# Cross-attention kernel: the second half of a tile's output projection runs in one piece ahead of the next tile's output transposes

## The reference

```
query = x @ Wq;  keyt = enc @ Wk;  valt = enc @ Wv
hs = mha(query, keyt, valt)                  # 2048 rows against 150 keys
ca_q1 = einsum('btc,th->bch', ca, Wq_ca)[:, indices, :]
ca_hs1 = mha(ca_q1, x, x)
ca_hs2 = mha(ca_hs1 @ Wq, ca @ Wk_ca, ca @ Wv_ca)
out = (hs + ca_hs2) @ Wout + b_out + x
```

## Time and profile before

| what | value |
|---|---|
| time, median of 3 runs | 1592.3 us (1591.59 to 1593.23) |
| the profiled execution, own time | 1591.01 us |
| its span, first to last instruction | 1589.2 us |
| PE busy | 1530.4 us, 96% of the span |
| PEld busy | 1254.2 us, 79% |
| DVE busy | 789.6 us, 50% |
| ACT busy | 623.4 us, 39% |
| mean granted TensorE clock | 0.99 |

### The profile page before, as it was taken

How to read it: one execution, slowest core, us unless ns; L and a number is a source line. 1 busy time by engine, 2 the same in 40 slices (tenths; PEclk the granted TensorE clock), 3 DMA queues, 4 the chain that set the end, 5 groups by cost and what they waited for, 6 DMA issues and landing times.

```text
span 1589.2 us, 24605 instructions
## 1 busy us (share of the span) xinstructions
PE 1530.4 (96%) x10294; PEld 1254.2 (79%) x10294; DVE 789.6 (50%) x1591; ACT 623.4 (39%) x1314; POOL 2.8 (0%) x12
## 2 busy tenths in 40 slices
PE   5999999999999999999999999999999999999999
PEld 4774589999976369999987538999998744899998
DVE  5677345343368543533447825334344782443533
ACT  1426723233143852322324484223233357332322
POOL 0000000000000000000000000000000000000000
PEclk9989999999999999999999999999999999999999
DMA  6530002130234001112025200114004510021101
GB/s 238 193 131 34 1 23 88 55 118 20 98 134 151 1 6 56 64 67 94 26 100 186 91 1 18 52 56 152 18 34 143 179 38 1 19 92 55 59 17 42
DMA packets 46680, 117.27 MB, mean 74 GB/s; under 512 B 3661, under 2 KB 5317, under 8 KB 45019
## 3 DMA queue, kind: packets, MB, share of 16 engines
q1 hardware_dynamic: 37036, 93.91, 16.8%
q10 hardware_dynamic: 9535, 21.80, 3.6%
HBM read 77.33 MB, written 39.17 MB: 73 GB/s over the span
## 4 chain that ended last, share of the span: by engine, by line
PE 82%; ACT 7%; DVE 7%; issue 2%; DMA 1%; SPq 0%; ACTq 0%
PE ps_w L492 41%; PE ps_s L492 17%; PE ps_t L492 15%; PE ps_t L502 9%; DVE unit_max L1247 4%; ACT work L1070 3%; ACT work L1040 1%; DVE ot L1413 1%; ACT ot L1102 1%; DMA xc<-in_L_xattn_Wout_dram 1%; ACT ot L986 0%; DMA y_all<-in_L_xattn_Wv_ca_dram 0%; PE ps_s L502 0%; PE ps_w L502 0%; ACT work L974 0%
## 5 line engine op out<-in xcount | busy, mean ns | idle before, releaser
L492 PE MATMUL ps_w<-wo_h,ot 128*128 128x320 f32 x1280 | 327.2, 321 | 1.0 <-DVE ot L1413 1.0
L1247 DVE TENSOR_REDUCE unit_max<-ps_s 128x1 f32<-128x512 f32 x384 | 239.8, 683 | 53.4 <-PE ps_s L492 52.6
L492 PEld LDWEIGHTS ps_w<-wo_h,ot 128*128 128x128 f32 x1280 | 222.5, 188 | 2.0 <-DVE ot L1413 2.0
L492 PE MATMUL ps_w<-wo_l,ot 128*128 128x320 f32 x640 | 197.7, 309 | 0.0
L1040 ACT ACTIVATE work<-ps_s,neg_max 128x150 f32<-128x150 f32 x512 | 161.0, 400 | 41.8 <-DVE neg_max L1305 41.8
L492 PE MATMUL ps_w<-v_all,work 120*128 120x162 f32 (+1 forms) x1280 | 171.3, 288 | 0.0
L492 PEld LDWEIGHTS ps_w<-v_all,work 120*128 120x128 f32 x1280 | 169.1, 191 | 0.8
L1031 ACT ACTIVATE work<-ps_t 120x512 f32<-120x512 f32 (+1 forms) x128 | 62.9, 491 | 226.1 <-PE ps_t L502 226.1
L502 PE MATMUL ps_t<-ident,work 128*120 128x128 f32 (+1 forms) x960 | 139.9, 276 | 2.0 <-DVE ot L1413 1.0
L492 PE MATMUL ps_s<-keys_h,qt_h 128*128 128x300 f32 (+1 forms) x448 | 134.8, 301 | 0.6
L1301 DVE TENSOR_REDUCE neg_max<-ps_s 128x6 f32<-128x900 f32 x64 | 70.1, 1095 | 126.9 <-PE ps_s L492 126.9
(11 more groups left out here) (159 smaller groups left out, 2230.1 us busy)
## 6 DMA issues: line engine op xcount, KB each, us to landing
xc<-in_x_dram SPq DMA_DIRECT2D x32, 1280.0 KB, 6.4
out_dram<-work ACTq DMA_DIRECT2D x64, 320.0 KB, 2.2
xt_all<-work SPq DMA_DIRECT2D x60, 256.0 KB, 2.2
xt_l<-xt_all SPq DMA_DIRECT2D x12, 1280.0 KB, 5.6
y_all<-in_L_xattn_Wk_dram SPq DMA_DIRECT2D x4, 960.0 KB
y_all<-in_L_xattn_Wv_dram SPq DMA_DIRECT2D x4, 960.0 KB
pick<-pick_all SPq DMA_DIRECT2D x16, 194.0 KB
xc<-in_L_xattn_Wq_dram SPq DMA_DIRECT2D x1, 1600.0 KB, 10.6
```

The costliest lines, as they stand in the source:

```text
L492: return nc.tensor.matmul(out, lhs, rhs, start=start, stop=stop, skip_group_check=True)
L1247: v.tensor_reduce(unit_max[:, a, n, q:q + 1], bank, AX_X, ALU.max).then_inc(max_free, 1)
```

## The change

In ten tiles of sixteen (s = 1, 3, 4, 5, 7, 8, 9, 11, 12, 13) the whole second half of the projection of tile s - 1 is issued first, and the five transposes of `turn_o(s)` come behind it. Tiles 2, 6, 10, 14 (where t is `GATHER_AT`) and 15 keep the old order, and tile 0 has none. No other engine's list changes, and no instruction is added or removed.

```diff
--- before.py
+++ after.py
@@ -920,12 +920,13 @@
                         tile_scores(2, (0,))
                         turn_o(0)
                         tile_scores(2, (1, 2))
-                    if s:
+                    if s and (t == GATHER_AT or s == SLOTS - 1):
                         project(s - 1, 1, range(0, 2))
-                    if s:
                         turn_o(s)
-                    if s:
                         project(s - 1, 1, range(2, KT))
+                    elif s:
+                        project(s - 1, 1)
+                        turn_o(s)
                 project(SLOTS - 1, 0)
                 project(SLOTS - 1, 1)
```

## The result

The changed kernel took 1585.1 us in the median of seven runs (1582.6 to 1588.0), beside 1592.3 us for the kernel before (1591.2 to 1593.6, seven runs): ratio 0.9957, interval 0.9945 to 0.9968. It is faster, and by more than the forecast 1588.5 us; it lies outside the range. The profiled execution took 1586.3 us against 1591.0, a span of 1584.4 against 1589.2 us. So one profile gained 4.8 us and the medians 7.2 us, where 3.8 were forecast. Three numbers for one change are the question of this document.

A forecast was written before the change was run, and what follows sets the result against it. PE, busy 96% of the span, was taken to bound the kernel. Removing 40 waits of 0.095 us gives 3.8 us, all else nothing: 1592.3 - 3.8 = 1588.5 us, range 1586.3 to 1591.1.

The forecast's parts named there:

- The wait, its place and its size: At `turn_o` in ten tiles, four batches: PE's wait for DVE's normalise goes in 40 places, 3.8 us gained.
- The choice of 0.095 us between 0.04 and 0.15: Gain per place at `turn_o`: 0.04 is only the late start, 0.15 adds a whole weight load; 0.095 compares whole stretches.
- the rival with the small gain: At `turn_o`: only the late start is gained, or part returns at another wait; 1.6 us or less, chance 0.12.
- the one with the whole load exposed: At `turn_o`: the transposes' weight load had been exposed whole; gain 6.0 us, to 1586.3 us, chance 0.07.
- The neighbours and the queues: Transposes followed directly by scores, and DMA issues that go out later: both put at no cost.
- the base of the sum: The unchanged kernel's median of 1592.3 us, from three runs differing by 1.6 us, from which 3.8 was subtracted.
- 0.6 us for the spread of medians: Whole kernel: spread allowed around the forecast time, used for the 0.64 chance of measuring below 1589.1 us.
- the granted clock is at 2.4 GHz but for the start: Whole kernel, read from the profile page: no slow clock in the loop over the tiles to win back.

The follow-up runs named there:

- margin run: The changed kernel with two unread 384-column additions on VectorE ahead of `ot_l` in the ten tiles; 1589.8 us, 3.9 above the changed kernel.

## Why the prediction was wrong

**The wait, its place and its size: right.** The stretch fell from 0.68 to 0.59 us in the changed tiles and stayed in the others; a changed tile takes 11.65 us; the tiles gave 3.9 us in the profile where the text had 3.8. The choice of 0.095 us between 0.04 and 0.15 was right: a start put off by 0.04 us costs 0.1, and the rows show with it a weight load that comes out from under the matmul. The margin run shows the same at another wait, 0.06 us late and 0.11 us dear. That the load is the reason is read from these rows and was not tested apart. By the 3.9 us of the tiles both the rival with the small gain (1.6) and the one with the whole load exposed (6.0) are out.

**The neighbours and the queues: right.** Transposes followed by scores cost nothing, `ot_l` ended 0.80 us ahead (0.75 forecast), and none of the later DMA issues shows in the tiles.

**The step that failed is the base of the sum**, "1592.3 - 3.8 = 1588.5" with "0.6 us for the spread of medians". It took three runs for the kernel's median. Executions of the kernel before spread over 14 us with the clock, around 1589.5; the three had fallen within 1.6 us, near 1592. From 1589.5 the sum gives 1585.7, and the changed kernel's 19 runs have a mean of 1585.5. So of the 7.2 us of the first comparison 3.9 are the change, 2.8 a base that stood high and did not come back, and 0.5 the changed kernel's own seven runs. Why the base stood high stays open, as said above. Seven runs a side of one comparison did not cover this spread; the interval of 0.9945 to 0.9968 was too narrow for it.

Behind it stands a reading of the clock that was wrong. That "the granted clock is at 2.4 GHz but for the start" is false: in that very trace each of the three batch boundaries has 3.4 us at 1.2 GHz, and batch 0 has 10.2 us of it from 100.5 us on (the one 8 in the row). That "there is no slow clock in the loop over the tiles to win back" was true, but I took it for the whole kernel. The page's clock row is too coarse for this: a slice is 40 us long, and a stretch of 3.4 us at half clock in it still prints as 9. Windows over a batch's first part would have shown 0.99, and over the boundary 0.52.

## What to carry to other kernels

On an engine that is busy throughout, read starts, not idle time: a start only 0.04 us late behind another engine's end cost 0.1 us, with the weight load laid open too, and three matmuls moved ahead of it were enough to win that back. Move such a step only where what follows it has cover; in the five tiles a batch without it the same move cost 1.35 us a place. Before a difference of 0.2% is read off medians, look at the mean clock of each run and at windows of a few us around the stage boundaries, and compare the stage that was changed by itself.

## What the runs showed of the hardware that was not expected

The same 1032 matmuls of a batch's first part took 157.6, 159.1 and 163.0 us in one execution, by how much of them ran at 1.2 GHz. Of the 49 slow stretches behind the first 60 us and ahead of the last tile 0, in fifteen profiles, 17 begin just behind a batch boundary, where PE was busy for 1.9 to 2.6 us of the 3.5 us before (2.0 of 3.6 in the window above). The other 32 begin behind 3.5 us of which PE was recorded busy for 3.16 to 3.40. In the two of them shown here, of the changed kernel, it is a mix of 512-column, 56-column and 12-row matmuls, in the first with transposes; the top two rows are the same place as the middle two, one batch earlier. Columns as above:

```profile
480.99:484.49 3.50, 3.16 (x20) 2.02 (x18) 2.89 (x6) 0.98 (x2) 0.00 (x0) 1.00 0.20 75
484.49:494.99 10.50, 10.32 (x55) 7.51 (x55) 7.32 (x14) 2.77 (x5) 0.00 (x0) 1.00 0.55 180
...
866.00:869.50 3.50, 3.16 (x20) 2.02 (x18) 2.89 (x6) 0.98 (x2) 0.00 (x0) 1.00 0.20 75
869.50:880.00 10.50, 10.50 (x37) 8.01 (x37) 6.20 (x12) 1.57 (x3) 0.00 (x0) 0.51 0.56 178
...
1258.60:1262.10 3.50, 3.40 (x16) 2.18 (x17) 3.48 (x6) 0.00 (x0) 0.00 (x0) 1.00 0.94 266
1262.10:1265.50 3.40, 3.40 (x9) 2.65 (x9) 0.85 (x4) 0.98 (x2) 0.00 (x0) 0.50 0.78 268
```

In batches 1 and 2 the same instructions stand in the 3.5 us, with the same busy times on every engine, and behind them the clock falls in batch 2 and not in batch 1. So the busy share that the trace records does not tell where the clock falls.

The Trainium skill, "TensorE: Matmul & The Clock Gate", section "What's actually happening", says of the slow matmuls at a kernel's start that their number differs from run to run of one kernel. Two profiles of the changed kernel agree: over the first 60 us their granted clock is 0.91 and 0.89. Here the slow stretches lie in the middle of the kernel too, and the kernel before spreads over 14 us with the clock. Eleven matmuls a batch whose results nobody reads (four in the first batch) made the changed kernel over 7 us faster, though which places to fill was found by trying and not from a rule.
